# Filled waits of the tensor engine, a later turn for q and spread loads of FFN weights in a two-layer gated cross-attention kernel

## The reference, cut to what matters

```python
x = x + tanh(g_xattn[0]) * L0_xattn(layernorm(x), ctx)   # 32 heads of 128, 8 kv heads, RMS-normed q and k
x = x + tanh(g_ffn[0])   * L0_ffn(layernorm(x))          # 8 routed low-rank experts, rank 16
x = x + tanh(g_xattn[1]) * L1_xattn(layernorm(x), ctx)   # 16 heads of 96, 4 kv heads, no norm of q and k
x = x + tanh(g_ffn[1])   * L1_ffn(layernorm(x))          # 512 -> 1792 gate and up, silu, -> 512
# in each attention
kv = concatenate([ctx, latents])                          # 256 rows of keys and values
q, k, v = latents @ Wq, kv @ Wk, kv @ Wv
out = softmax(q @ k.T * scale) @ v                        # 4 query heads share one kv head
return out @ Wo
```

## Time and profile before

| what | value |
|---|---|
| median of 3 runs | 1152.05 us (1151.71 to 1152.43) |
| the profiled execution's own time | 1151.04 us |
| its span | 1149.2 us |
| PE busy | 1117.6 us, 97% |
| ACT / DVE / POOL busy | 837.8 / 829.5 / 377.8 us |
| mean granted clock of the PE | 0.995 |

### The profile page before, as it was taken

One profiled execution on the slowest core, in us unless ns is written; L12 is line 12 of the kernel. 1 busy time (PEld: TensorE's weight loads), 2 busy tenths in 40 slices (PEclk: granted clock), 3 DMA queues, 4 the chain that ended last, 5 costly groups with the idle time before them and its releaser, 6 DMA issues.

```text
span 1149.2 us, 22754 instructions
## 1 busy us (share of the span) xinstructions
PE 1117.6 (97%) x7160; PEld 706.1 (61%) x7160; DVE 829.5 (72%) x1996; ACT 837.8 (73%) x2759; POOL 377.8 (33%) x674
## 2 busy tenths in 40 slices
PE   7789999999999999999999999899999999899998
PEld 5456665666566656665666666667667666455554
DVE  5878777777767767777687878887778788744444
ACT  6978888888888888888887777788787776522221
POOL 5663434336633343333335443212121212110000
PEclk8999999999999999999999999999999999999999
DMA  7676654554655645656364675778987695310000
GB/s 255 136 156 117 136 139 117 127 115 110 135 143 97 144 122 132 141 93 161 85 132 93 106 148 113 153 133 194 226 183 151 134 188 110 82 28 1 37 1 37
DMA packets 418328, 141.13 MB, mean 123 GB/s; under 512 B 392993, under 2 KB 402977, under 8 KB 418209
## 3 DMA queue, kind: packets, MB, share of 16 engines
q1 hardware_dynamic: 416304, 136.01, 54.6%
q0 software_dynamic: 1904, 3.67, 1.2%
HBM read 39.21 MB, written 2.10 MB: 36 GB/s over the span
## 4 chain that ended last, share of the span: by engine, by line
PE 78%; DVE 10%; issue 3%; POOL 3%; ACT 3%; DMA 2%; SPq 0%; DVEq 0%; POOLq 0%; ACTq 0%
PE bank L599 22%; PE bank L601 22%; PE bank L600 22%; PE bank L801 8%; PE bank L820 5%; DVE pieces L1179 2%; DVE mx L1280 1%; DVE stats L1190 1%; DVE x L1315 1%; ACT probs L998 1%; ACT junk L895 1%; POOL rstd L1583 1%; DMA k_weight<-in_k_norm_w 1%; DVE q_rows L1179 1%; DVE oT L1179 1%
## 5 line engine op out<-in xcount | busy, mean ns | idle before, releaser
L998 ACT ACTIVATE probs<-bank,nb,rq 128x256 f32<-128x256 f32 x256 | 141.4, 564 | 40.8 <-DVE nb L1285 39.8
L1179 DVE SCALAR_TENSOR_TENSOR pieces<-probs,rs,pieces 128x256 f16<-128x256 f32 x384 | 166.6, 493 | 4.9 <-ACT pieces L892 2.5
L892 ACT ACTIVATE pieces<-probs,rs 128x256 f16<-128x256 f32 x384 | 166.1, 522 | 2.8 <-DVE rs L1295 0.8
L1280 DVE TENSOR_REDUCE mx<-bank 128x2 f32<-128x512 f32 x192 | 131.1, 683 | 47.8 <-PE bank L601 47.4
L895 ACT ACTIVATE junk<-bank 128x128 bf16<-128x128 f32 x384 | 101.7, 288 | 45.4 <-PE bank L601 44.4
L599 PE MATMUL bank<-wq,xT 128*128 128x512 f16 (+1 forms) x352 | 126.7, 360 | 0.0
L601 PE MATMUL bank<-wq,xT 128*128 128x512 f16 (+1 forms) x352 | 126.6, 360 | 0.0
L600 PE MATMUL bank<-wq,xT 128*128 128x512 f16 (+1 forms) x352 | 126.6, 360 | 0.0
L599 PE MATMUL bank<-wo,oT 128*128 128x512 f16 x320 | 121.3, 379 | 2.8 <-DVE oT L1179 2.3
L1179 DVE SCALAR_TENSOR_TENSOR q_rows<-bank,q_rows 128x512 f16<-128x512 f32 (+1 forms) x96 | 62.1, 646 | 82.3 <-ACT junk L895 79.7
L601 PE MATMUL bank<-wo,oT 128*128 128x512 f16 x320 | 121.3, 379 | 0.0
(11 more groups left out here) (218 smaller groups left out, 2804.4 us busy)
## 6 DMA issues: line engine op xcount, KB each, us to landing
raw_o<-in_wo_a SPq DMA_DIRECT2D x8, 1024.0 KB, 6.3
raw_q<-in_wq_a SPq DMA_DIRECT2D x7, 1024.0 KB, 6.0
raw_kv<-in_wkv_a SPq DMA_DIRECT2D x8, 512.0 KB, 4.4
turned<-pieces SPq DMA_TRANSPOSE x192, 2.8
raw_q<-in_wq_c SPq DMA_DIRECT2D x4, 768.0 KB, 4.9
raw_o<-in_wo_c SPq DMA_DIRECT2D x4, 768.0 KB, 5.1
down_rest<-in_down_t POOLq DMA_DIRECT2D x5, 512.0 KB, 4.0
ff_in<-in_gate_t SPq DMA_DIRECT2D x4, 448.0 KB, 3.8
```

The lines of the kernel that those rows point to most:

```text
L892: return act.activation(out, in_, ACT.Copy, scale=scale)
L998: act.activation(probs[:, h, :], bank[h // 2][:, (h % 2) * KV:(h % 2 + 1) * KV], ACT.Exp, bias=nb[:, h:h + 1], scale=scale, accum_out=sums ...
L1179: return dve.scalar_tensor_tensor(out, in_, scale, hi, ALU.mult, ALU.subtract)
L1280: dve.tensor_reduce(mx[:, pr], chunks(bank[i][:, :], 2), AX.X, ALU.max, negate=True).then_inc(mx_done, 1)
```

## The change

It has four parts.

1. `awake` is now a matmul of `ones` (16-bit, 128 columns) by itself instead of a transpose of the 32-bit identity, and writes to a bank that is given. There are 52 of them before the PE's first work, which now wait for the second constant only, 28 in place of the 10 before the first `kv_proj`, and four new places: 22 before the second source of step 3's keys, 32 before the scores of step 1, 24 before the projection of step 0 and 32 before the values of step 1. In the last two places waits are put in another order, so that the fill comes after the bank is free and ahead of the wait that is long.
2. In layer 1 (n from 64) SP's list has q's turn behind the two turns of the probabilities.
3. The eight loads of the gate and up weights go from steps 70 to 77 to steps 71, 73, 75, 76, 78, 79, 82 and 83.
4. The two first loads of the down weights go from steps 72 and 74 to 81 and 84.

```diff
+FF_LOADS = (71, 73, 75, 76, 78, 79, 82, 83)
+DOWN_LOADS = (81, 84)
@@ SP, step(n)
-                if T < N:
-                    turn_k(T)
-                if T < N - 1:
-                    turn_q(T)
-                if S < N:
-                    turn(S, 0)
-                    turn(S, 1)
+                if n < N0:
...
+                else:
+                    if T < N:
+                        turn_k(T)
+                    if S < N:
+                        turn(S, 0)
+                    if S < N:
+                        turn(S, 1)
+                    if T < N - 1:
+                        turn_q(T)
...
-                if 70 <= n < 70 + 2 * KC:
-                    i, k = divmod(n - 70, KC)
+                if n in FF_LOADS:
+                    i, k = divmod(FF_LOADS.index(n), KC)
@@ PE
-            def awake(n):
+            def awake(n, out):
                 for _ in range(n):
-                    pe.transpose(bank[4][:, 0:P], ident[:, :], ident[:, :])
+                    pe.matmul(out[:, 0:P], ones[:, :], ones[:, :], start=True, stop=True)
@@ kv_proj
                 for i in sources:
+                    if n == 3 and i == 1:
+                        awake(22, kv_bank(n))
@@ scores
+                if n == 1:
+                    awake(32, kv_bank(3))
                 pe.wait_ge(kturned, 16 * (n + 1))
@@ values
-                for i in range(2):
-                    pe.wait_ge(pturned[i], 16 * (n + 1))
...
                 if n >= 1:
                     pe.wait_ge(olo_done, n)
+                if n == 1:
+                    awake(32, bank[4])
+                for i in range(2):
+                    pe.wait_ge(pturned[i], 16 * (n + 1))
@@ project
+                if n == 0:
+                    pe.wait_ge(kn_done, 8)
+                    awake(24, y_bank(n))
                 pe.wait_ge(olo_done, n + 1)
...
-                if n == 0:
-                    pe.wait_ge(kn_done, 8)
@@ the PE's opening
+            pe.wait_ge(consts, 2)
+            awake(52, bank[4])
             pe.wait_ge(consts, 5)
-            awake(22)
...
-            awake(10)
+            awake(28, bank[4])
             kv_proj(0, (1,), last=False)
@@ POOL, step(n)
-                if n in (72, 74):
-                    m = n - 72
+                if n in DOWN_LOADS:
+                    m = 2 * DOWN_LOADS.index(n)
```

## The result

| | median us | lowest to highest | runs |
|---|---|---|---|
| before | 1152.28 | 1150.03 to 1152.95 | 11 |
| changed | 1155.49 | 1152.16 to 1159.99 | 11 |

The profiled execution took 1154.04 us (span 1152.2), 3.0 us more than that of before.

What follows compares the result with a forecast made beforehand. PE, streaming matmuls nearly without pause, was taken as the bound. 1151.04 - 2.0 (opening) - 0.8 (q's order and loads together) = 1148.2 us, with the runs' 1.0 us offset a median of 1149.2; range 1147.0 to 1152.0.

Steps and rivals of the forecast that it cites:

- The opening: Projections from 13.34 us: full clock ends the second 2.4 us earlier, of which 2.0 us were taken as gain.
- That takes a clock that has already fallen, which in these places it never had: Four later fills: overrunning their waits by 3.3 us together needs half clock, held never to occur there; cost taken as 0.
- the rule of transposes: Skill's rule that PE-mode transposes don't raise the clock; by it 2.4 us almost sure, but the prediction argued the trace contradicts it.
- The 6 in 10 for a clock that holds: Chance given that the clock is up at 13.34 us, after a pause of 2.4 us, and the opening's gain arrives.
- The wait of step 79: PE's 0.81 us wait for turned probabilities at 860.93 us; order and moved loads together remove it once, -0.8 us.
- 1.3 us earlier removes it: Layer 1: probabilities' turns issued 1.3 us earlier, ahead of q's, end PE's 0.81 us wait; bounds 0 and -1.0.
- The loads: Moved gate, up and down loads of the FFN: no cost; their gain is the same 0.8 us, counted once.
- the cost of q's later turn: Layer 1, ACT's next `q_hi`: loop 7.6 us by the median, 9.9 by the slowest, against step's 8.5; cost taken as 0.
- The prediction's own limit, a landing of 4.3 us: The slower rival decides from a landing of q's turn of 8.5 - 4.15 = 4.3 us on.
- The slower rival: q's later turn becomes the bound at ACT's `q_hi`, load steps 71 to 84: 1153.0 to 1157.2 us, chance 0.08.

Runs made afterwards that it cites:

- e_q_loads: Changed kernel without any of the opening's new fills (old 22 and 10 transposes back), q's later turn and moved loads kept: 1156.73 us against 1151.97 before, 1.004.
- e_open_q: Changed kernel with the FFN's loads back in their old steps, fills and q's later turn kept: 1154.71 us, 1.0032 to the kernel before.
- e_two_rows: Changed kernel with two buffers for q's rows used in turn, SP's order as changed: 1147.88 us, 0.9972 to the kernel before.
- e_rest_late: Changed kernel with POOL's five `down_rest` loads all in step 92 instead of steps 85 to 89: 1163.53 us against 1152.36 before, 1.0098.

## Why the prediction was wrong

**The opening: right.** The two projections ran at full clock, as forecast, and the gain arrived: 2.0 us were taken, and 2.8 in the median (1.6 to 4.6) came. The trace that the term was read from shows one execution, and its fall was a long one: in the four other profiles with the old 22 and 10 transposes step 8 ended 0.8 to 1.2 us earlier than in it, in the eight with all of the change's fills 2.2 to 4.2 us earlier. "That takes a clock that has already fallen, which in these places it never had" held for the execution read and not for others: without the four later fills the clock fell there in four of five profiles, with them in none of eleven, so these fills secure more than was thought. In arguing against the rule of transposes the prediction overlooked that eight more transposes and two sums of squares ran between the 22 and the 10. The 6 in 10 for a clock that holds was about what was seen, 6 of 9 profiles.

**The wait of step 79: gone, but not by the later turn alone.** Step 79 alone brought 1.04 us in the profiled pair (from 3.41 us ahead at the end of step 78 to 4.45 at the end of 79), against 0.8. "1.3 us earlier removes it" is not borne out: in the profile of e_q, with only the order changed, PE still waits in that step, 0.95 us ahead of the output projection and 0.16 us ahead of the product with the turned probabilities. In the profile of e_loads, with only the loads moved, the wait is gone, and the step brings the same 1.04 us. In the medians neither is seen (0.9999 and 1.0001).

**The loads: right by themselves**, 1.0001.

**The step that failed** is the cost of q's later turn: "ACT is busy for 72.69 of 90 us, which leaves it 1.6 us a step, so a turn that is 1.4 us late is absorbed. I take 0". ACT's idle time is outside the loop. ACT waits for the landing, the landing waits for SP, SP waits for DVE's low pieces, and these come after ACT has written the q; what an engine has free elsewhere in the step doesn't shorten a circle of waits. A circle longer than the step slips by the difference each time round, and that adds up. Its length was nearly right: 4.15 us to the issue, 4.58 measured. Its landing was taken from the wrong place: the median of 3.4 us belongs to 760 to 850 us, and the loads that make it 4.5 to 5.1 are issued in steps 85 to 89. In the trace of before q's landings between 905 and 950 us already had a median of 3.7:

```profile
DMA to landing us min/median/max: 2.8/3.7/3.9
```

With that and its own 4.15 the prediction would have had 7.9 us of 8.5, with the 4.58 that were measured it is 8.3, a loop with 0.2 us to spare. The prediction's own limit, a landing of 4.3 us, was right to within 0.4 us (8.48 - 4.58 = 3.9).

**The slower rival** had the mechanism and the price (1153 to 1157 us), but the wrong place, steps 71 to 84. The losses lie in steps 82 to 92: 1.6 us of the 7.7 are lost from the end of step 81 to that of 84, 3.5 in 86 to 91, and 2.6 in 92, where the steps become shorter and what had slipped can't be hidden any more. Its chance of 0.08 rested on loads "which are spread now"; only SP's loads are spread, not POOL's.

**The sum of parts.** Opening 0.9973, order 0.9999, loads 1.0001: multiplied 0.9973, measured together 1.0037, which is 7.4 us apart. That the order causes it, through the one buffer, is shown by the runs with the order undone and with a second buffer. Why it stays free alone can be read from the traces. In the profile of e_q, at the same place as the changed kernel's loop above:

```profile
928.04 0.48 ACT L902 ACTIVATE q_rows<-bank 128x384 f16<-128x384 f32 x1
...
932.66 0.57 ACT L902 ACTIVATE v_hi<-bank,alpha 128x96 f16<-128x96 f32 x2 [1.27 <-PE bank L611]
932.79 1.26 SPq L493 DMA_TRANSPOSE q_half<-q_rows  x1
...
934.68 0.74 POOL L1775 DMA_DIRECT2D down_rest<-in_down_t  x1
```

The same in the changed kernel, where its q was written at 929.69 us and its turn issued at 934.27:

```profile
932.76 0.55 ACT L916 ACTIVATE v_hi<-bank,alpha 128x96 f16<-128x96 f32 x2
...
934.75 0.74 POOL L1789 DMA_DIRECT2D down_rest<-in_down_t  x1
```

POOL issues its load after the pieces of k, for which it waits on ACT, which makes them after v. While ACT is on time, it waits 1.27 us for PE there, the load comes 1.4 to 1.9 us behind q's turn, and the four turns of e_q with a load behind them land in 2.7 to 3.7 us. Once ACT is late, PE's bank is already full and that wait is gone. Load and turn then both follow from ACT's write of q. They come within 0.7 us of each other, the turn takes 4.5 to 5.1 us, and that makes ACT late for the next one.

So once it is entered this state holds itself as long as POOL has a load in every step, and something else has to bring it in. At 910 us ACT's wait for q was already 1.1 us in the changed kernel and 1.3 in e_q_loads; in both a turn beside the moved down load of step 81 had taken over 5 us, but that the one comes from the other isn't shown. In the kernel with fills and old loads (e_open_q) there was no wait at 910 us. There the first late turn was that of step 86, which took 4.9 us with its load 1.9 us behind, and the same distance left 3.7 us or less in e_q. So the holding is read from the traces, and what tips the loop no run isolates.

## What to carry to other kernels

When a transfer moves back in a queue, find the buffer that it frees and add up the whole circle, from the write into it to the next write, with the landing as it is beside the busiest transfers of any engine. If the circle with its slowest landing is longer than a step, give it a second buffer; idle time of the engines in it is no reserve. Parts that are each harmless can be dear together, so time the combination. And where the matrix engine's pause is filled for the clock's sake, fill every such wait that follows as well, and look at more than one execution: a pause that one execution gets through drops the clock in the next.

## What the runs showed of the hardware

The upper level of the clock came while PE ran nothing but the 22 transposes: in the profiled execution of the kernel before, PE began four or five of them in each half microsecond up to 5.5 us, and six in the next. The Trainium skill, "TensorE: Matmul & The Clock Gate", Part 4, has transposes not counting as busy in the same way, and the full clock not coming on with them. This case's trace disagrees. How far they count stays open: in e_q's profile the clock fell again in the tenth microsecond (mean 0.59), and the ten transposes of 2.38 us that followed ran at half clock.

A pause of the same length is followed by a fall in one execution and not in the next: 2.08 us (changed kernel, 1.00 after it) against 2.07 us (e_two_rows, 0.50 after it). The changed kernel's executions spread over 7.8 us, more than twice the gain that was looked for.

A transposing DMA on SP's queue is slowed by a 512 KB load from POOL's queue beside it. In the profiles of the changed kernel, e_q_loads and e_open_q eleven turns of q had one of the `down_rest` loads within 0.7 us and took 4.5 to 6.7 us to land; with no load near, turns mostly take 2.8. It isn't so of every load: one of the first down weights, 0.47 us behind a turn (e_rest_late, step 81), left it at 2.8 us.
